# Wide attention of a fused transformer kernel: products of 128 rows by 128 columns gathered in every other slot

## The chip, the cores and the metric

The kernel runs on one core of a Trainium2 chip. The time is the device time of one execution in microseconds; smaller is better. A core has TensorE (matrix products; its weight loads run beside them), VectorE, ScalarE, GpSimd and SyncE, each with its own queue that it works through in program order. They wait for each other through semaphores.

## The reference, cut to what matters

Six layers are computed on x of 16 x 256 x 128. The change touches only the first, an attention with 16 heads of 64:

```python
q = (x @ Wq).reshape(b, s, N_HEADS, HEAD_DIM)
k = (x @ Wk).reshape(b, s, N_HEADS, HEAD_DIM)
v = (x @ Wv).reshape(b, s, N_HEADS, HEAD_DIM)
dot = jnp.einsum('bihd,bkhd->bhik', q, k)
w = jax.nn.softmax(dot / jnp.sqrt(jnp.float32(HEAD_DIM)), axis=-1)
a = jnp.einsum('bhij,bjhd->bihd', w, v)
a = a.reshape(b, s, N_HEADS * HEAD_DIM)
return a @ Wo + bo
...
x = x + _L0_attn_a_ref(_layernorm(x, axis=-1), L0_attn_a_Wq, L0_attn_a_Wk, L0_attn_a_Wv, L0_attn_a_Wo, L0_attn_a_bo)
```

## The kernel before

The wide attention takes the 16 batches one after the other, and the 16 heads of a batch as 8 pairs. A batch has 8 slots, one for each pair, and `wide_slots` lists what stands in a slot as (name, index, batches ahead). `wide_walk` repeats this list for all batches, and every engine walks through the same list in the same order and does its own part of each entry. So the order of this one list is the order of every queue. The entries are:

- norm: TensorE turns the normalized x of a batch (two transposes, 128x128), ScalarE copies them out. xn is ScalarE's normalizing ahead of it.
- qk: queries and keys of one pair, two float32 products with w_q and w_k, each in two passes, 128 rows by 128 columns; ScalarE copies both (128x512) to the SBUF, and GpSimd makes a bfloat16 copy for "max".
- v: a quarter of the values (128x128, 512 wide), copied out by ScalarE.
- max: approximate scores in bfloat16 (64 rows by 128 columns), of which VectorE takes the row maxima. split and turnmax: VectorE splits the maxima of a batch in three bfloat16 parts, TensorE turns them (128x128), VectorE copies the result to `shift`. The first score of the batch waits for this copy.
- score: the shift (`pick` times `shift`) and the exact scores (64x128), then ScalarE's exponential; GpSimd adds the two key tiles.
- value and sum: products of 128 rows by 64 columns into the banks Ob; divide: VectorE's reciprocal and multiplication.
- project: eight products with w_o (128x128; float32, so 16 passes), which VectorE adds to x, and takes the moments for the next layer.

The entries norm, qk, v, project and turnmax share the two PSUM banks 6 and 7, strictly in turn: the bank is the entry's place in the list modulo 2. A filling waits until the filling before it in the same bank has been copied out (`drained`).

```python
    for what, i, _ in slots:
        if what in ("norm", "qk", "v", "project", "turnmax"):
            bank[what, i] = len(bank) % 2
```

In a slot i the list has: divide of pair i-2, score of pair i, max of pair i+1 of the next batch, value and sum of pair i-1, and then the 128x128 products; slot 6 has the split behind its max, and slot 7 the turnmax and its products ahead of value and sum. On VectorE the two additions of the projections stand in slots 3 and 5, each behind that slot's divide and maximum.

Of the kernel before, what the change touches and what calls it, by code (L numbers as in the profile page):

```python
# [243 lines left out]
PAIRS = H // 2  # L244
# [1684 lines left out]
def wide_slots():  # L1929
    slots = []  # L1930
    for i in range(PAIRS):
        slot = [("divide", (i - 2) % PAIRS, -1 if i < 2 else 0), ("score", i, 0)]
        slot += [("max", (i + 1) % PAIRS, 2 if i + 1 >= PAIRS else 1)]
        slot += [("split", 0, 1)] if i == 6 else []
        slot += [("turnmax", 0, 1)] if i == 7 else []
        products = [("qk", (i + 3) % PAIRS, 2 if i + 3 >= PAIRS else 1)]
        products += {1: [("v", 0, 1)], 2: [("v", 1, 1), ("xn", 0, 2)], 3: [("project", 0, -1)],
                     4: [("v", 2, 1), ("norm", 0, 2)], 5: [("project", 1, -1)], 6: [("v", 3, 1)]}.get(i, [])
        values = [(what, (i - 1) % PAIRS, -1 if i < 1 else 0) for what in ("value", "sum")]
        slots += slot + (products + values if i == 7 else values + products)  # L1940
    return slots


def wide_walk():

    slots, order, counts = wide_slots(), [], [0, 0]
    bank = {}
# [3 lines that stand above are left out]
    for n in range(-2, NB + 1):  # L1951
        for what, i, ahead in slots:
            if 0 <= n + ahead < NB:
                m = bank.get((what, i))
                if m is not None:
                    counts[m] += 1
                order.append((what, i, n + ahead, m, counts[m] if m is not None else None))
    return order
# [376 lines left out]
```

## Time and profile before

| | us |
|---|---|
| median of 3 runs | 2353.46 (2351.25 to 2359.56) |
| the profiled execution | 2350.0 |
| its span in the trace | 2348.3 |
| TensorE busy in the span | 2052.1 (87%) |
| VectorE busy | 1544.7 (66%) |
| ScalarE busy | 1199.0 (51%) |
| GpSimd busy | 825.0 (35%) |

Busy times are sums over six layers with different limits, so that they say little about one of them. The wide attention is read from stretches within its first 655 us. Matmul ends are modelled in the trace, so distances are taken from start to start. "128*64 128x256" in a row is a matmul of 128 rows by 64 columns of the array with 256 columns streamed. "x8" means that eight instructions in a row were merged, and what stands in brackets is the idle time before them and who ended it.

### The profile page before, as it was taken

The page shows a single profiled execution, that of the slowest core. Times are in us where ns is not written, and L with a number is a line of the kernel's source. Part 1 is how long each engine was busy: PE and PEld are TensorE (multiplying, and loading weights), DVE is VectorE, ACT ScalarE, POOL GpSimd, SP SyncE. Part 2 cuts the span into 40 slices and gives each one's busy share as a digit, 9 for nine tenths or more (in the row PEclk, how much of TensorE's full clock was granted, in tenths as well). Part 3 has the DMA queues.
Part 4 walks back from the last instruction along what each step waited for, and adds up shares of the span by engine and source line. Part 5 has one row for each costly group of instructions (what it writes and reads, how often), then busy time and mean ns, then how long its engine had stood idle before and what let it go on. Part 6 is the DMA issues. An engine that isn't in the chain of part 4 may idle for free. (4 is left out here: it accounts for less than half of the span.)

```text
span 2348.3 us, 52692 instructions
## 1 busy us (share of the span) xinstructions
PE 2052.1 (87%) x20735; PEld 1381.5 (59%) x20735; DVE 1544.7 (66%) x2742; ACT 1199.0 (51%) x2044; POOL 825.0 (35%) x1272
## 2 busy tenths in 40 slices
PE   6999999999959997998689989997599985479996
PEld 3666666666648995555578966664345543335553
DVE  5777777777743435666354447774688875768884
ACT  3444444444343324665623326655477776447774
POOL 4444444444423432332144414441233322433330
PEclk9999999999969998999789989998699997769998
DMA  5000000000000022444000214441244420134441
GB/s 167 1 1 1 1 1 1 1 1 1 1 6 2 14 46 70 113 113 99 2 4 1 55 29 113 113 112 32 70 100 115 113 61 1 42 80 107 113 109 46
DMA packets 142787, 120.97 MB, mean 52 GB/s; under 512 B 11808, under 2 KB 127408, under 8 KB 142548
## 3 DMA queue, kind: packets, MB, share of 16 engines
q1 hardware_dynamic: 142548, 117.64, 21.1%
q8 instruction: 167, 2.74, 0.5%
q14 instruction: 72, 0.59, 0.1%
HBM read 63.48 MB, written 54.12 MB: 50 GB/s over the span
## 5 line engine op out<-in xcount | busy, mean ns | idle before, releaser
L906 DVE TENSOR_REDUCE l_group_mx<-maxima 128x4 f32<-128x1024 f32 x248 | 304.0, 1226 | 69.0 <-PE maxima L699 67.5
L834 ACT ACTIVATE l_group_pr<-scores 128x1024 f32<-128x1024 f32 x256 | 261.5, 1021 | 71.7 <-PE scores L720 69.1
L2171 POOL TENSOR_TENSOR l_wide_tiles_sum<-l_wide_pr 128x256 f32<-128x256 f32 x256 | 180.7, 727 | 212.4 <-ACT l_wide_pr L2114 212.4
L2142 DVE RECIPROCAL l_wide_rc<-bank 128x256 f32<-128x256 f32 x128 | 223.8, 1749 | 8.4 <-PE bank L2075 7.9
L2114 ACT ACTIVATE l_wide_pr<-scores 128x512 f32<-128x512 f32 x256 | 139.1, 595 | 163.1 <-PE scores L2058 163.1
L2126 DVE TENSOR_REDUCE l_wide_mx<-maxima 128x2 f32<-128x512 f32 x248 | 159.4, 685 | 52.6 <-PE maxima L2038 52.0
L906 DVE TENSOR_REDUCE l_slope_mx<-maxima 128x6 f32<-128x768 f32 x124 | 118.9, 959 | 74.2 <-PE maxima L706 72.7
L2104 ACT ACTIVATE l_wide_qk<-bank 128x512 f32<-128x512 f32 x128 | 76.4, 597 | 175.2 <-PE bank L2025 175.2
L906 DVE TENSOR_REDUCE l_rope_mx<-maxima 128x6 f32<-128x768 f32 x124 | 118.8, 958 | 56.3 <-PE maxima L706 55.4
L834 ACT ACTIVATE l_slope_pr<-scores 128x768 f32<-128x768 f32 x128 | 103.5, 809 | 87.0 <-PE scores L727 86.8
L834 ACT ACTIVATE l_rope_pr<-scores 128x768 f32<-128x768 f32 x128 | 103.7, 811 | 77.0 <-PE scores L727 76.8
L740 PE MATMUL bank<-l_group_pr,va 128*32 128x256 f32 x2048 | 142.1, 397 | 0.0
L2069 PE MATMUL bank<-l_wide_pr,l_wide_va 128*64 128x256 f32 x1024 | 138.8, 392 | 0.0
L699 PE MATMUL maxima<-l_group_st 50*128 50x256 bf16 x992 | 101.8, 285 | 39.1 <-DVE l_group_mx L906 14.4
L2058 PE MATMUL scores<-l_wide_qk 64*128 64x256 f32 x1024 | 131.4, 376 | 0.0
L2166 POOL CAST l_wide_qk<-l_wide_qk 128x512 bf16<-128x512 f32 x128 | 78.1, 610 | 146.2 <-ACT l_wide_qk L2104 146.2
L1001 POOL CAST l_group_cols<-l_group_mx 128x32 bf16<-128x32 f32 x32 | 6.7, 209 | 318.8 <-DVE l_group_mx L906 318.8
L720 PE MATMUL scores<-l_group_st 53*128 53x256 bf16 x1024 | 102.6, 279 | 16.3 <-ACT l_group_pr L834 11.5
L2058 PEld LDWEIGHTS scores<-l_wide_qk 64*128 64x128 f32 x1024 | 98.6, 189 | 9.8
L1660 ACT ACTIVATE l_rope_e_ht<-maxima 128x512 f32<-128x512 f32 x64 | 38.2, 597 | 106.4 <-PE maxima L1612 106.0
L2025 PE MATMUL bank<-l_wide_xnt,w_q 128*128 128x256 f32 x256 | 90.3, 435 | 2.5 <-ACT l_wide_qk L2104 1.4
L1660 ACT ACTIVATE l_slope_e_ht<-maxima 128x512 f32<-128x512 f32 x64 | 38.2, 597 | 104.4 <-PE maxima L1612 104.1
(468 smaller groups left out, 4853.5 us busy)
## 6 DMA issues: line engine op xcount, KB each, us to landing
l_group_st<-stack_dram SPq DMA_DIRECT2D x64, 384.0 KB, 5.5
l_slope_st<-stack_dram SPq DMA_DIRECT2D x32, 384.0 KB, 5.6
l_rope_st<-stack_dram SPq DMA_DIRECT2D x32, 384.0 KB, 5.5
stack_dram<-l_group_parts SPq DMA_DIRECT2D x64, 192.0 KB, 2.3
stack_dram<-l_group_parts SPq DMA_DIRECT2D x64, 128.0 KB, 1.9
stack_dram<-l_slope_parts SPq DMA_DIRECT2D x32, 192.0 KB, 2.4
stack_dram<-l_rope_parts SPq DMA_DIRECT2D x32, 192.0 KB, 2.3
stack_dram<-l_slope_parts SPq DMA_DIRECT2D x32, 128.0 KB, 2.3
```

Of the source, the lines that this page charges most:

```text
L699: ins = pe.matmul(Mx[:, z, first:first + keys], st[at, b % KEEP, 0, i, t * P:(t + 1) * P], st[at, b % KEEP, 1, i, 0:keys], start=(t == 0 o ...
L720: ins = pe.matmul(Tp[:, z, t * S:t * S + S - first], st[at, b % KEEP, 1, i, t * P:(t + 1) * P], st[at, b % KEEP, 0, i, first:S], start=(t ...
L740: ins = pe.matmul(Ob[i // 2][32 * z:32 * z + 32, (i % 2) * S + first:(i % 2) * S + S], va[:, b % KEEP, t, h // G, :], pr[:, (h // 2) % AHE ...
L834: act.activation(pr[:, i % AHEAD, :, 0:keys], Tp[:, :, 0:keys], ACT.Exp).then_inc(s["exps"], 1)
L906: dve.tensor_reduce(mx[:, b % 2, :, :, i], max_bank(i, b)[:, :, 0:BLOCKS * keys].rearrange("p z (a k) -> p z a k", k=keys), AX.X, ALU.max, ...
L2025: ins = pe.matmul(bank[:, z * S:(z + 1) * S], w[:, i * P:(i + 1) * P], xnt[:, at, :], start=True, stop=True)
L2058: ins = pe.matmul(Tb[z][:, t * S:(t + 1) * S], qk[rows(z), at, i, 1, t * P:(t + 1) * P], qk[rows(z), at, i, 0, :], start=False, stop=(t == ...
L2069: ins = pe.matmul(Ob[i % 2][rows(z), 0:S], va[:, at, kt, 2 * i + z, :], pr[:, i % 2, z, kt * S:(kt + 1) * S], start=(kt == 0), stop=(kt == ...
L2114: act.activation(pr[:, i % 2, z, :], Tb[z][:], ACT.Exp).then_inc(s["exps"], 1)
L2126: dve.tensor_reduce(mx[:, at, :, 2 * i + z], max_banks(i, b)[z][:].rearrange("p (t k) -> p t k", k=S), AX.X, ALU.max, negate=True).then_in ...
L2142: own.done(dve.reciprocal(rc[:], Ob[i % 2][:, S:2 * S]))
L2171: pool.tensor_tensor(tiles_sum[:, i % 2, z, :], pr[:, i % 2, z, 0:S], pr[:, i % 2, z, S:2 * S], ALU.add).then_inc(s["added"], 1)
```

## The change

The list of `wide_slots` is written differently. Slots 1, 3 and 5 have no qk, v, norm or project any more, nor has slot 7 a qk. Slots 0, 2, 4 and 6 have the qk of two pairs each. The normalizing for two batches ahead moves from slot 2 to slot 0, the quarters of v from slots 1, 2, 4 and 6 to 0, 2, 4 and 6, and both projections of the batch before, from slots 3 and 5, to slot 6: one as the first product of the row, the other as the last. Nothing else is changed; each engine has as many instructions as before. The changed file is four lines longer, so that its line numbers behind this place are higher by 4.

```diff
--- before.py
+++ after.py
@@ -1933,9 +1933,13 @@
         slot += [("max", (i + 1) % PAIRS, 2 if i + 1 >= PAIRS else 1)]
         slot += [("split", 0, 1)] if i == 6 else []
         slot += [("turnmax", 0, 1)] if i == 7 else []
-        products = [("qk", (i + 3) % PAIRS, 2 if i + 3 >= PAIRS else 1)]
-        products += {1: [("v", 0, 1)], 2: [("v", 1, 1), ("xn", 0, 2)], 3: [("project", 0, -1)],
-                     4: [("v", 2, 1), ("norm", 0, 2)], 5: [("project", 1, -1)], 6: [("v", 3, 1)]}.get(i, [])
+
+        products = []
+        if i % 2 == 0:
+            products = [("qk", j % PAIRS, 2 if j >= PAIRS else 1) for j in (i + 3, i + 4)]
+            products = {0: [("xn", 0, 2), ("v", 0, 1)] + products, 2: products[0:1] + [("v", 1, 1)] + products[1:2],
+                        4: [("norm", 0, 2), ("v", 2, 1)] + products, 6: [("project", 0, -1), ("v", 3, 1)] + products}[i]
+            products = (products + [("project", 1, -1)]) if i == 6 else products
         values = [(what, (i - 1) % PAIRS, -1 if i < 1 else 0) for what in ("value", "sum")]
         slots += slot + (products + values if i == 7 else values + products)
     return slots
```

TensorE, from the end of slot 5 to slot 7 of a batch, before (l0_wide_xnt with w_q and w_k is qk, w_v with it is v, w_o is the projection, parts the turned maxima, pr and tiles_sum are value and sum), beginning with the projection in slot 5:

```order
L2083 MATMUL bank7<-w_o,l0_wide_att_t 128x128 x8
L2054 MATMUL scores<-l0_wide_shift,pick 128x512 x2
L2058 MATMUL scores<-l0_wide_qk 128x256 x4
L2038 MATMUL maxima<-l0_wide_qk16 128x256 x4
L2069 MATMUL bank5<-l0_wide_pr,l0_wide_va 64x256 x4
L2075 MATMUL bank5<-l0_wide_tiles_sum,ones 64x256 x2
L2025 MATMUL bank6<-l0_wide_xnt,w_q 128x256
L2025 MATMUL bank6<-l0_wide_xnt,w_k 128x256
L2031 MATMUL bank7<-w_v,l0_wide_xnt 128x512
L2054 MATMUL scores<-l0_wide_shift,pick 128x512 x2
L2058 MATMUL scores<-l0_wide_qk 128x256 x4
L2038 MATMUL maxima<-l0_wide_qk16 128x256 x4
```

And in the change, slot 6, from behind its "sum" up to slot 7's first value product:

```order
L2087 MATMUL bank6<-w_o,l0_wide_att_t 128x128 x8
L2035 MATMUL bank7<-w_v,l0_wide_xnt 128x512
L2029 MATMUL bank6<-l0_wide_xnt,w_q 128x256
L2029 MATMUL bank6<-l0_wide_xnt,w_k 128x256
L2029 MATMUL bank7<-l0_wide_xnt,w_q 128x256
L2029 MATMUL bank7<-l0_wide_xnt,w_k 128x256
L2087 MATMUL bank6<-w_o,l0_wide_att_t 128x128 x8
L2058 MATMUL scores<-l0_wide_shift,pick 128x512 x2
L2062 MATMUL scores<-l0_wide_qk 128x256 x4
L2042 MATMUL maxima<-l0_wide_qk16 128x256 x4
L2050 MATMUL bank7<-ident16,parts 128x128 x2
L2073 MATMUL bank4<-l0_wide_pr,l0_wide_va 64x256 x4
```

Before, one projection stands in slot 5, slot 6 has the two products of a qk and a v, and the scores of slot 7 follow the v; behind the turn of parts came slot 7's qk. In the change the row of slot 6 has both projections with v and two qk between, the second projection stands directly ahead of slot 7, and slot 7 has no qk behind the turn of parts.

VectorE, slots 5 to 7, before (TENSOR_TENSOR x is the addition of a projection, RECIPROCAL with the line after it the divide, maxima the maximum, shift the copy that the next batch's score waits for), beginning with that addition in slot 5:

```order
L2148 TENSOR_TENSOR x<-x,bank7 128x128
L2150 BN_STATS moments<-x 128x6
L2142 RECIPROCAL l0_wide_rc<-bank4 128x256
L2143 TENSOR_TENSOR l0_wide_att_t<-bank4,l0_wide_rc 128x256
L2126 TENSOR_REDUCE l0_wide_mx<-maxima 128x2 x2
L2132 CAST parts<-l0_wide_mx 128x4x16
L2133 TENSOR_TENSOR l0_wide_mrest<-l0_wide_mx,parts 128x32
L2134 CAST parts<-l0_wide_mrest 128x4x16
L2135 TENSOR_TENSOR parts<-l0_wide_mrest,parts 128x4x16
L2142 RECIPROCAL l0_wide_rc<-bank5 128x256
L2143 TENSOR_TENSOR l0_wide_att_t<-bank5,l0_wide_rc 128x256
L2126 TENSOR_REDUCE l0_wide_mx<-maxima 128x2 x2
```

And in the change, beginning with the last instruction of the split in slot 6:

```order
L2139 TENSOR_TENSOR parts<-l0_wide_mrest,parts 128x4x16
L2152 TENSOR_TENSOR x<-x,bank6 128x128
L2154 BN_STATS moments<-x 128x6
L2152 TENSOR_TENSOR x<-x,bank6 128x128
L2154 BN_STATS moments<-x 128x6
L2146 RECIPROCAL l0_wide_rc<-bank5 128x256
L2147 TENSOR_TENSOR l0_wide_att_t<-bank5,l0_wide_rc 128x256
L2130 TENSOR_REDUCE l0_wide_mx<-maxima 128x2 x2
L2142 COPY l0_wide_shift<-bank7 128x256
L2146 RECIPROCAL l0_wide_rc<-bank4 128x256
```

The addition that stood ahead of slot 6's divide stands now, with the other one, behind slot 6's split; the divide, the maximum and the copy to shift of slot 7 follow it.

## Rows read from the trace of the kernel before

**Rows 1.** Busy time by stretch; columns: stretch, its length, busy us and instructions, clock, DMA
```profile
core 0: us, PE busy (x) PEld busy (x) DVE busy (x) ACT busy (x) POOL busy (x), PEclk, DMA share, GB/s
100.00:200.00 100.00, 99.34 (x736) 64.14 (x733) 77.28 (x110) 42.89 (x79) 43.42 (x65) 1.00 0.00 1
```

**Rows 2.** Timeline of TensorE, slots 5 (end), 6 and 7; start us, length us
```profile
302.62 1.95 PE L2083 MATMUL bank<-w_o,l_wide_att_t 128*128 128x128 f32 x16
304.50 0.39 PE L2054 MATMUL scores<-l_wide_shift,pick 64*128 64x512 bf16 x2
...
305.90 1.08 PE L2069 MATMUL bank<-l_wide_pr,l_wide_va 128*64 128x256 f32 x8
...
307.35 0.70 PE L2025 MATMUL bank<-l_wide_xnt,w_q 128*128 128x256 f32 x2
307.88 0.59 PE L2025 MATMUL bank<-l_wide_xnt,w_k 128*128 128x256 f32 x2
308.31 1.02 PE L2031 MATMUL bank<-w_v,l_wide_xnt 128*128 128x512 f32 x2
309.27 0.39 PE L2054 MATMUL scores<-l_wide_shift,pick 64*128 64x512 bf16 x2
...
310.79 0.65 PE L2025 MATMUL bank<-l_wide_xnt,w_q 128*128 128x256 f32 x2
...
311.80 1.08 PE L2069 MATMUL bank<-l_wide_pr,l_wide_va 128*64 128x256 f32 x8
312.72 0.60 PE L2075 MATMUL bank<-l_wide_tiles_sum,ones 128*64 128x256 f32 x4
313.54 0.39 PE L2054 MATMUL scores<-l_wide_shift,pick 64*128 64x512 bf16 x2 [0.22 <-DVE l_wide_shift L2138]
```

**Rows 3.** Timeline of TensorE, the next batch's first score
```profile
352.46 0.39 PE L2054 MATMUL scores<-l_wide_shift,pick 64*128 64x512 bf16 x2 [0.22 <-DVE l_wide_shift L2138]
```

**Rows 4.** Timeline of VectorE, slots 6 and 7
```profile
304.67 0.29 DVE L2148 TENSOR_TENSOR x<-x,bank 128x128 f32<-128x128 f32 x1 [3.07 <-PE bank L2083]
...
305.20 1.74 DVE L2142 RECIPROCAL l_wide_rc<-bank 128x256 f32<-128x256 f32 x1
...
308.63 0.20 DVE L2132 CAST parts<-l_wide_mx 128x64 bf16<-128x64 f32 x1
...
309.89 1.74 DVE L2142 RECIPROCAL l_wide_rc<-bank 128x256 f32<-128x256 f32 x1
...
313.20 0.28 DVE L2138 COPY l_wide_shift<-bank 128x256 bf16<-128x256 bf16 x1
```

**Rows 5.** Timelines of ScalarE, weight loads (PEld) and TensorE around a transpose, slot 2
```profile
336.70 0.60 ACT L2104 ACTIVATE l_wide_qk<-bank 128x512 f32<-128x512 f32 x1 [1.56 <-PE bank L2025]
...
337.35 0.20 PEld L2019 LDWEIGHTS bank<-ident,l_wide_xn 128*128 128x128 f32 x2 [0.66 <-ACT l_wide_qk L2104]
...
336.50 1.02 PE L2031 MATMUL bank<-w_v,l_wide_xnt 128*128 128x512 f32 x2
337.36 0.43 PE L2019 MATMUL bank<-ident,l_wide_xn 128*128 128x128 f32 x2
337.72 0.39 PE L2054 MATMUL scores<-l_wide_shift,pick 64*128 64x512 bf16 x2
```

**Rows 6.** Timeline of TensorE in the last batch, without products
```profile
622.13 0.39 PE L2054 MATMUL scores<-l_wide_shift,pick 64*128 64x512 bf16 x2 [0.52 <-DVE l_wide_shift L2138]
...
624.23 0.60 PE L2075 MATMUL bank<-l_wide_tiles_sum,ones 128*64 128x256 f32 x4
624.76 0.39 PE L2054 MATMUL scores<-l_wide_shift,pick 64*128 64x512 bf16 x2
```

**Rows 7.** Waits of TensorE in the fill, 20 to 50 us; total us, times, longest
```profile
PE bank L2025 <- ACT l_wide_qk L2104: 1.4, 3, 0.7
PE bank L2025 <- ACT l_wide_xnt L2101: 0.9, 2, 0.5
```

**Rows 8.** Timeline of TensorE at the end of the fill
```profile
43.93 0.39 PE L2038 MATMUL maxima<-l_wide_qk 64*128 64x256 bf16 x4
...
45.90 0.39 PE L2054 MATMUL scores<-l_wide_shift,pick 64*128 64x512 bf16 x2
```

## The prediction

> **What bounds the kernel now.** I read three views in this order. First the busy time of each engine over stretches of the span: while the wide attention runs, TensorE has work in 99.3 us of 100, at the full granted clock, and VectorE in 77, ScalarE and GpSimd in 43 each [rows 1]. So this layer, the first 655 us of the 2348.3 us span, goes at TensorE's pace; DMA is idle in it, and nothing behind it is touched by the diff. Second the timeline of TensorE over the end of one batch [rows 2]. One batch takes 38.92 us, from 313.54 to 352.46 [rows 2, 3]. The reader is to see which blocks follow with a gap. A slot is "score" with "max" 1.40 us (304.50 to 305.90), "value" with "sum" 1.45 (305.90 to 307.35), then the products of 128x128. Third VectorE's timeline [rows 4]: from 304.67 on no row shows a pause, and the copy of the turned maxima at 313.20 is what TensorE waits for: the score products of the next batch start only at 313.54.
>
> **What a change of shape costs.** A block of w_q products lasts 0.53 us where it is the first behind a 64-column product (307.35 to 307.88), and the w_k block, the same size, 0.43 [rows 2]. So entry costs 0.10: the load of weights had no matmul of its own kind to hide under. A v block lasts 0.86 us before another 128x128 product (336.50 to 337.36) and 0.96 before a score (308.31 to 309.27) [rows 2, 5]: leaving costs 0.10. "sum" lasts 0.53 before a score too when nothing stands between (624.23 to 624.76, no wait) [rows 6], against 0.43 for its four products as a w_k block has them, so that step from 128x64 to 64x128 costs the same 0.10. The Trainium skill, TensorEngine Tiling (Array Packing), section Key Properties, says that a change of tiling mode drains the engine; the trace agrees, at 0.10 us a time.
>
> **The change, step by step, for one batch.** Slots 1, 3 and 5 lose their 128x128 products. Each then goes "sum" to "score" directly, and one entry and one leaving are gone: 3 x 0.20 = -0.60 us. The products themselves are all still there.
> Slot 7 keeps the turn of the maxima but loses its qk: those took 1.01 us (310.79 to 311.80) where 0.86 is the bare time and 0.10 the leaving, which stays: -0.05.
> The old wait in front of slot 0: "sum" has 0.82 us there where 0.53 would do (slot 7 lasts 4.27 us, 309.27 to 313.54; its parts are 1.52 for score, max and turn, 309.27 to 310.79, then 1.01 and 1.45, in sum 3.98): -0.29 [rows 2].
> New late weight loads. The products have two banks, taken in turn, and in slots 0, 2, 4 and 6 a third product now needs a bank that ScalarE has just emptied, with only one product of 0.86 us between. The trace has this pattern once a batch: ScalarE ends its copy at 337.30, the load of weights starts at 337.35 and the matmul at 337.36, which is just where it would have been [rows 5]. So no full wait comes, but the load has no lead, and a load without lead costs a 128x128 float32 product 0.10, as at the entry. With a lead of 0.01 to 0.02 I take 0.09 for each of four: +0.36 (bounds 0 and 0.40). The old case was a transpose, whose block is 0.36 (337.36 to 337.72) with 0.10 of leaving, where two passes of 0.11 (a projection is 16 such in 1.78) would be bare: 0.05 is saved there, and 0.05 as the transpose now takes the entry: -0.10. In slot 6 the fifth product has a longer row ahead of it and is free.
> A price by the page alone: the Trainium skill, TensorE: Matmul & The Clock Gate, section LDWEIGHTS, gives columns / 1.2 ns, which is 107 ns for 128 columns; with it the four would be 0.43 instead of 0.36.
>
> **The moved projections.** This is the step that decides. VectorE adds the two projections to x in program order. Before, they stood in slots 3 and 5, and VectorE sat 3.07 us ahead of each [rows 4], with time to catch up. Now both stand in slot 6, the second as the last product of it. VectorE finishes the first, and then must wait about 4 us (v and two qk, 0.86 each, and the second projection, 1.88 with the leaving from 302.62 to 304.50, so 1.78) with the divide of pair 5 behind it, whose operands lie ready. Behind that divide stand the maximum and the copy of the turned maxima, for which TensorE's next batch waits. I count from the start of slot 7, where the second projection is just done. Its add starts 0.17 later (304.67 against 304.50); add and statistics 0.53 (to 305.20); divide and maximum 3.31 (309.89 to 313.20); copy to TensorE's start 0.34 (to 313.54) [rows 2, 4]. Sum 4.35 us. TensorE's own slot 7 is then 1.52 + 0.10 (leaving the turn) + 1.45 = 3.07. So it waits 4.35 - 3.07 = +1.28 us ahead of slot 0.
>
> Elsewhere VectorE has cover: a pair costs it 3.31 us, an odd slot is now 1.40 + 1.45 = 2.85, but an even one 5.6 or more, and the next slot's divide never has to be done before the slot after. ScalarE's two exponentials (1.1 us a slot) and GpSimd's sums keep pace in such short slots: 624.76 is 2.63 us behind the score before it without a wait (622.13 and 624.76) [rows 6].
>
> Sum for a batch: -0.60 - 0.05 - 0.29 + 0.36 - 0.10 + 1.28 = **+0.60 us**. It holds for 13 batches (those with a projection in them and two batches ahead to fill): +7.8 us.
>
> **The edges.** Fill before the first score: TensorE waited 1.4 + 0.9 us there for ScalarE's copies [rows 7], 0.7 of it because two qk in a row took the same bank, which now alternate; with other products between, I take the 2.3 as gone, and 0.8 for four switches less (4 x 0.20). Against it: from the last "max" of the fill to the first score (43.93 to 45.90) [rows 8] VectorE's maximum and copy hid a qk of 0.9 us, now nothing. -2.3 + 0.9 - 0.8 = -2.2 (bounds -4 and 0; a clock that rises earlier or later is not counted). First batch, without projections and without the wait: -0.4. The last two: fewer switches and a shorter VectorE chain: -1.0. Edges: -3.6.
>
> **Total** +7.8 - 3.6 = +4.2 us on the profiled execution's 2350.0: 2354.2. Its 2350.0 lies 3.5 below the median of the three runs, 2353.46; with that, I predict 2357.7 us. What a measurement of this kernel can tell from no change is about 0.3%, 7.1 us.
>
> **Rivals.**
> A. The gain without the price: VectorE is done with the divide of pair 5 in time, so that slot 7 has no wait. For it: VectorE is busy only 77% [rows 1]. Against it: the order of its queue, in which nothing passes the second projection. A batch would be -0.60 - 0.05 - 0.29 + 0.36 - 0.10 = -0.68, in all -8.8 - 3.6 = -12.4: 2341. Chance 0.08. The Trainium skill, TensorEngine Tiling (Array Packing), section Key Properties, by which each change of mode that falls away is a drain less, speaks for this case and not for the wait.
> B. Slower, past 0.3%: VectorE is late for the first projection as well. It can start the divide of pair 4 0.1 into slot 6 ("sum" of slot 5 ends 1.40 + 0.92 + 0.60 into it), and has 3.31 and 1.26 to do (the split of the maxima, 308.63 to 309.89) [rows 4]: free at 4.7. The first projection is ready for it at 5.0 (2.85 + 0.10 + 1.78, and 0.27 for the end of its last product), and its bank is wanted again at 5.6, when the add of 0.29 is done. So there are 0.3 us to spare; every tenth beyond costs TensorE a tenth in every batch. With ScalarE's copies also late by 0.1 in four places it is +0.5 a batch: +6.5, 2364. Decides from 0.3 us of lateness. Chance 0.24.
> C. The late loads cost nothing (TensorE's queue holds the load back less than at an entry): +0.24 a batch, +3.1 - 3.6 = -0.5: 2353. Chance 0.16.
> D. The change does not remove switches: excluded by the order of rows and by 624.23 to 624.76 [rows 6].
> My forecast has 0.52.
>
> **How the numbers follow.** The forecast itself spreads by the fill (2 us either way) and by three runs that differ among themselves by 8 us. From +4.2 with such a spread (about 4 us) a quarter of its 0.52 passes +7.1, which is 0.13; with nearly all of B's 0.24 less 0.06 that stay inside, slower is 0.31. Faster is A and a little of C: 0.11. Within 0.3%: 0.58. The range leaves out A and the far end of B: 2347 to 2366.
>
> **What would show each step.** In the changed profile: a wait of TensorE at the first score product of a batch on VectorE's copy of shift, "idle before" 1.2 us (0.22 now), 14 times; a wait of VectorE of about 4 us ahead of one add to x in each batch, the other nearly none; odd slots of 2.85 us; no wait at the third product of a row, but its first pass 0.1 us longer; a batch of 39.5 us against 38.92; a first score at about 44 instead of 45.90. A batch under 38.5 us would prove A, one over 40 B. The prediction is wrong in its main step if VectorE's idle time ahead of its second add does not exceed 3 us.

## The result, and the profile after

The changed kernel takes 2360.78 us (median of 20 runs, 2352.96 to 2365.99), the kernel before 2354.07 (20 runs, 2349.57 to 2363.78). The medians differ by 6.7 us. The ratio of the means (2360.40 and 2354.96) is 1.0023, with a 95% interval of 1.0013 to 1.0034: 5.4 us more (3.1 to 8.0), within the 0.3% that were called no change, but clear of zero. The profiled execution has a span of 2360.4 us.

The busy shares in the layer have fallen, TensorE's from 99.3 [rows 1] to 96.3 us in 100, at the full clock:

```profile
core 0: us, PE busy (x) PEld busy (x) DVE busy (x) ACT busy (x) POOL busy (x), PEclk, DMA share, GB/s
100.00:200.00 100.00, 96.33 (x722) 62.88 (x721) 72.25 (x107) 41.64 (x78) 41.81 (x62) 1.00 0.00 1
```

TensorE's timeline from the end of slot 6 to the first score of the next batch, and the score one batch later:

```profile
308.26 1.95 PE L2087 MATMUL bank<-w_o,l_wide_att_t 128*128 128x128 f32 x16
310.14 0.39 PE L2058 MATMUL scores<-l_wide_shift,pick 64*128 64x512 bf16 x2
...
311.55 0.28 PE L2050 MATMUL bank<-ident,parts 128*128 128x128 bf16 x2
311.76 1.08 PE L2073 MATMUL bank<-l_wide_pr,l_wide_va 128*64 128x256 f32 x8
312.67 0.60 PE L2079 MATMUL bank<-l_wide_tiles_sum,ones 128*64 128x256 f32 x4
314.50 0.39 PE L2058 MATMUL scores<-l_wide_shift,pick 64*128 64x512 bf16 x2 [1.22 <-DVE l_wide_shift L2142]
```

```profile
354.04 0.39 PE L2058 MATMUL scores<-l_wide_shift,pick 64*128 64x512 bf16 x2 [1.22 <-DVE l_wide_shift L2142]
```

The first score waits 1.22 us where it waited 0.22 [rows 2]; slot 7 lasts 4.36 us (310.14 to 314.50), and a batch 39.54 (314.50 to 354.04) instead of 38.92. VectorE, the same place:

```profile
305.85 0.29 DVE L2152 TENSOR_TENSOR x<-x,bank 128x128 f32<-128x128 f32 x1 [0.54 <-PE bank L2087]
...
310.32 0.29 DVE L2152 TENSOR_TENSOR x<-x,bank 128x128 f32<-128x128 f32 x1 [3.85 <-PE bank L2087]
...
310.85 1.74 DVE L2146 RECIPROCAL l_wide_rc<-bank 128x256 f32<-128x256 f32 x1
...
314.16 0.28 DVE L2142 COPY l_wide_shift<-bank 128x256 bf16<-128x256 bf16 x1
```

Its first addition of a projection finds the engine idle for 0.54 us, the second for 3.85. From the second on, it has no pause: 0.53 us to the divide at 310.85, 3.31 to the copy at 314.16, 0.34 to the score. That answers to [rows 4], where the same chain began one slot earlier. Over 13 batches, the waits (total us, times, longest) are:

```profile
DVE x L2152 <- PE bank L2087: 57.0, 26, 3.8
...
PE scores L2058 <- DVE l_wide_shift L2142: 15.9, 13, 1.2
```

The third product in slot 0, whose bank ScalarE has just emptied, and the qk ahead of it:

```profile
318.31 0.59 PE L2029 MATMUL bank<-l_wide_xnt,w_q 128*128 128x256 f32 x2
318.74 0.59 PE L2029 MATMUL bank<-l_wide_xnt,w_k 128*128 128x256 f32 x2
319.17 0.69 PE L2029 MATMUL bank<-l_wide_xnt,w_q 128*128 128x256 f32 x2
319.69 0.59 PE L2029 MATMUL bank<-l_wide_xnt,w_k 128*128 128x256 f32 x2
320.22 0.39 PE L2058 MATMUL scores<-l_wide_shift,pick 64*128 64x512 bf16 x2
```

The first w_q block lasts 0.43 us (318.31 to 318.74), the second 0.52 (319.17 to 319.69). The second one's load of weights starts at 319.15, when ScalarE's copy of v is done, 0.02 us ahead of its matmul; the next block's starts 0.21 us ahead (319.48 for 319.69). No idle time is reported, only the longer block: this is the late weight load. Slots 2, 4 and 6 have one such block each. In slots 4 and 6 it is the fourth product and not the third, as there v stands second and its copy frees the fourth product's bank.

The fill (the products ahead of the first score) ended earlier, and the last batch later. First score after the fill (45.90 before [rows 8]):

```profile
43.53 0.39 PE L2058 MATMUL scores<-l_wide_shift,pick 64*128 64x512 bf16 x2 [0.93 <-DVE l_wide_shift L2142]
```

The last projections, and the granted clock and busy times of their stretches:

```profile
645.14 2.05 PE L2087 MATMUL bank<-w_o,l_wide_att_t 128*128 128x128 f32 x16
647.64 2.05 PE L2087 MATMUL bank<-w_o,l_wide_att_t 128*128 128x128 f32 x16 [0.45 <-DVE x L2152]
...
657.22 0.49 PE L2087 MATMUL bank<-w_o,l_wide_att_t 128*128 128x128 f32 x2 [1.36 <-DVE l_wide_att_t L2147]
658.16 3.66 PE L2087 MATMUL bank<-w_o,l_wide_att_t 128*128 128x128 f32 x16 [0.45 <-DVE x L2152]
```

```profile
658.00:662.00 4.00, 3.66 (x16) 3.47 (x16) 0.47 (x3) 0.00 (x0) 0.00 (x0) 0.57 0.00 0
```

In the last two places the second projection waits 0.45 us for VectorE's addition of the first. The very last one runs at a granted clock of 0.57 (0.50, which is 1.2 GHz, from 659 to 661 us) and takes 3.66 us where the others take 2.05. The next layer's first instruction on VectorE is at 664.05 us, before the change at 656.55:

```profile
664.05 0.21 DVE L212 TENSOR_TENSOR mean<-moments 128x32 f32<-128x32 f32 x1 [1.50 <-PEq L2298]
```

```profile
656.55 0.21 DVE L212 TENSOR_TENSOR mean<-moments 128x32 f32<-128x32 f32 x1 [1.70 <-PEq L2294]
```

So the layer is 7.5 us longer in these two executions. What lies behind it is untouched by the change, and took 1696.4 us after (2360.4 - 664.05) and 1691.8 before.

### The profile page after: what moved, and what is told of

Its sections match the earlier page's. It is cut to its first block and busy times, and to the rows that moved or that the text cites. A ratio compares the mean times of both kernels' runs of the same rounds, so it can differ in the third digit from the quotient of the medians.

```text
span 2360.4 us, 52692 instructions
## 1 busy us (share of the span) xinstructions
PE 2046.0 (87%) x20735; PEld 1380.4 (58%) x20735; DVE 1537.7 (65%) x2742; ACT 1201.7 (51%) x2044; POOL 825.9 (35%) x1272
## 5 line engine op out<-in xcount | busy, mean ns | idle before, releaser
L2073 PEld LDWEIGHTS bank<-l_wide_pr,l_wide_va 128*64 128x64 f32 x1024 | 62.1, 136 | 45.4 <-issue 24.6
```

The lines of the kernel that those rows point to most:

```text
L2073: ins = pe.matmul(Ob[i % 2][rows(z), 0:S], va[:, at, kt, 2 * i + z, :], pr[:, i % 2, z, kt * S:(kt + 1) * S], start=(kt == 0), stop=(kt == ...
```

## The experiments

A batch is measured as in [rows 2, 3], from a first score to the next one, in the middle of the layer; it was the same to 0.01 us in all 13 inner batches of each kernel but the one of the turn behind the late projection, where the first of them was shorter. The table has them all; the middle column is the layer, up to the next layer's first VectorE instruction.

| kernel | a batch, us | end of the layer, us | time |
|---|---|---|---|
| before | 38.92 | 656.6 | 2354.07 |
| the change | 39.55 | 664.1 | ratio 1.0023 (1.0013 to 1.0034) |
| adjacent projections | 38.26 | 645.8 | ratio 0.9942 (0.9928 to 0.9957) |
| projections alone, adjacent | 38.63 | 650.9 | ratio 0.9973 (0.9960 to 0.9985) |
| projections alone, split | 39.09 | 656.9 | one run, 2355.4 |
| half v copies | 39.37 | 659.8 | one run, 2363.4 |
| turn in slot 6 | 38.15 | 643.7 | ratio 0.9939 (0.9916 to 0.9963) |
| turn behind the late projection | 38.56 | 649.2 | one run, 2346.6 |
| projections back | 38.65 | 650.3 | one run, 2348.1 |
| one switch added | 38.36 | 647.4 | one run, 2350.8 |

The single times scatter by several us, in stages that no edit touches; what a single run shows is its batch.

**Adjacent projections.** Against the change:

```diff
-                        4: [("norm", 0, 2), ("v", 2, 1)] + products, 6: [("project", 0, -1), ("v", 3, 1)] + products}[i]
-            products = (products + [("project", 1, -1)]) if i == 6 else products
+                        4: [("norm", 0, 2), ("v", 2, 1)] + products, 6: [("project", 0, -1), ("project", 1, -1), ("v", 3, 1)] + products}[i]
```

> The changed kernel with one thing different: in slot 6 the second projection stands directly behind the first, ahead of v and the two qk, and no longer as the last product of the row. Theory (VectorE is held at its second addition to x, and the divide, maximum and copy of shift queue behind it): VectorE's addition now comes 2.4 us before slot 7, its wait ahead of it falls from 3.85 to about 1.3 us, the copy of shift is done 2.97 us into slot 7 where TensorE needs 3.07, so the wait of 1.22 us at the first score of a batch goes to 0. A batch goes from 39.55 to 38.26 us, the two projections have different banks so that the last batch loses its 0.45 us waits as well, and the whole is 12 us under the kernel before: ratio 0.995. Rival 1 (the wait comes from the amount of VectorE's work in the short slots 5 to 7, not from its order): the batch stays at 39.4 to 39.55 us and the ratio at 1.002. Rival 2 (the gathered products do not save anything, the whole difference is in the projections): the batch comes back to 38.9 us, ratio 1.000.

Measured: a batch of 38.26 us and a ratio of 0.9942. VectorE and TensorE around slot 7:

```profile
303.05 0.29 DVE L2151 TENSOR_TENSOR x<-x,bank 128x128 f32<-128x128 f32 x1 [1.17 <-PE bank L2086]
...
303.58 1.74 DVE L2145 RECIPROCAL l_wide_rc<-bank 128x256 f32<-128x256 f32 x1
...
308.26 0.28 DVE L2141 COPY l_wide_shift<-bank 128x256 bf16<-128x256 bf16 x1
```

```profile
305.55 0.39 PE L2057 MATMUL scores<-l_wide_shift,pick 64*128 64x512 bf16 x2
...
308.62 0.39 PE L2057 MATMUL scores<-l_wide_shift,pick 64*128 64x512 bf16 x2
```

The second addition waits 1.17 us instead of 3.85, the divide starts at 303.58, before slot 7 begins (305.55), and slot 7 lasts 3.07 us without a wait. The whole 1.29 us are gone with the place of one product, with the same products on all engines. Both rivals fall: the amount of work is the same, and the batch is 0.66 us under that of before.

**Projections alone, adjacent.** Against the kernel before:

```diff
-        products += {1: [("v", 0, 1)], 2: [("v", 1, 1), ("xn", 0, 2)], 3: [("project", 0, -1)],
-                     4: [("v", 2, 1), ("norm", 0, 2)], 5: [("project", 1, -1)], 6: [("v", 3, 1)]}.get(i, [])
+        products += {1: [("v", 0, 1)], 2: [("v", 1, 1), ("xn", 0, 2)], 4: [("v", 2, 1), ("norm", 0, 2)]}.get(i, [])
+        products = [("project", 0, -1), ("project", 1, -1), ("v", 3, 1)] + products if i == 6 else products
```

> The kernel before (a qk in every slot, v where they were) with only the two projections moved: both as the first two products of slot 6. It has no gathering of the other products, but lacks the projections' own later place behind the qk. Theory: every switch of shape stays, as slots 3 and 5 still have a qk; VectorE is no longer late for the copy of shift, so the wait of 0.29 us ahead of slot 0 goes, and nothing else. A batch of 38.63 us against 38.92; about 4 us less in all, ratio 0.998. Rival (the projections are what matters, and gathering does nothing): a batch as short as that of the adjacent projections with gathering, 38.3 us. Together with that kernel it gives the worth of the gathering alone: the theory has 38.63 - 38.26 = 0.37 us a batch (0.60 + 0.05 - 0.36 + 0.10 by the prediction's terms).

Measured: 38.63 us a batch. Slot 7 of one:

```profile
306.89 0.39 PE L2054 MATMUL scores<-l_wide_shift,pick 64*128 64x512 bf16 x2
...
310.88 0.39 PE L2054 MATMUL scores<-l_wide_shift,pick 64*128 64x512 bf16 x2
```

3.99 us and no wait: only the old wait of 0.29 us is gone. So of the 0.66 us that adjacent projections with gathering have over the kernel before, 0.29 are this wait and 0.37 the gathering, as expected.

**Projections alone, split.** The same, with the second projection at the end of slot 6:

```diff
-        products = [("project", 0, -1), ("project", 1, -1), ("v", 3, 1)] + products if i == 6 else products
+        products = [("project", 0, -1), ("v", 3, 1)] + products + [("project", 1, -1)] if i == 6 else products
```

> The kernel before (a qk in every slot) with only the projections moved, as the change has them: one as the first product of slot 6, one as its last. Theory: VectorE's chain into slot 7 is the same 4.35 us as in the change, but TensorE's slot 7 still has its qk and lasts 3.98 us, so the wait ahead of slot 0 is 0.37 us where it was 0.29, and one late weight load adds 0.09: a batch of 39.09 us. So the place of the projections alone costs 0.2 us a batch, and it is the lost qk in slot 7 that lays the other 0.9 us of the wait bare. Rival (a projection at the end of the row costs its 1.2 us by itself): a batch of 40.1 us.

Measured: 39.09 us. Slot 7:

```profile
308.04 0.39 PE L2054 MATMUL scores<-l_wide_shift,pick 64*128 64x512 bf16 x2
...
312.39 0.39 PE L2054 MATMUL scores<-l_wide_shift,pick 64*128 64x512 bf16 x2 [0.30 <-DVE l_wide_shift L2138]
```

It lasts 4.35 us, as VectorE's chain does, and the wait in it is a small one, as slot 7's qk covers the rest. Against the adjacent projections, the late one costs 0.46 us in this neighbourhood (39.09 for 38.63): 0.36 in slot 7, and 0.09 of a late weight load in slot 6 (8.43 us for 8.34). In the change it costs 1.29 (39.55 for 38.26). The 1.29 need both edits, the late place and a slot 7 without its qk.

**Half v copies.** Against the change, from the third batch on; the kernel then leaves out half of each v, and the values there are those of an earlier batch:

```diff
-                    act.activation(va[:, at, i // 2, 8 * (i % 2):8 * (i % 2) + 8, :].rearrange("p h d -> p (h d)"),
-                                   Mb[m][:], ACT.Copy).then_inc(drained[m], 1)
+                    heads = 8 if b < 2 else 4
+                    act.activation(va[:, at, i // 2, 8 * (i % 2):8 * (i % 2) + heads, :].rearrange("p h d -> p (h d)"),
+                                   Mb[m][:, 0:64 * heads], ACT.Copy).then_inc(drained[m], 1)
```

> The changed kernel, but from the third batch on ScalarE copies only the first 4 of 8 heads of each v block out of its bank (256 columns instead of 512), so that half of the values stay those of an earlier batch; everything else is as in the change. Theory of the late weight loads: in slots 0, 4 and 6 the bank of the third product is then free 0.2 us earlier, its weight load has its lead, and its block falls from 0.52 to 0.43 us; slot 2, where the bank is freed by a qk's copy, keeps 0.52. A batch of 39.28 us against 39.55, with the wait of 1.22 us unchanged. Rival (the 0.52 us are the price of a third product in a row, whatever its bank): 0.52 everywhere and 39.55 us.

Measured: 39.37 us, a saving of 0.18 and not 0.27. The third product in slot 0:

```profile
317.49 0.59 PE L2029 MATMUL bank<-l_wide_xnt,w_k 128*128 128x256 f32 x2
317.92 0.59 PE L2029 MATMUL bank<-l_wide_xnt,w_q 128*128 128x256 f32 x2
318.36 0.59 PE L2029 MATMUL bank<-l_wide_xnt,w_k 128*128 128x256 f32 x2
```

Its w_q block (317.92 to 318.36) is down to 0.44. Slot 0 is 5.63 us (5.72 in the change), slot 4 5.81 (5.90), slot 2 unchanged at 5.73, as expected; slot 6 is 9.29 (9.30). There the last projection waits on the bank of the product two ahead of it: once the fourth product is not late any more, the fifth is (the projection's block is 1.97 us instead of 1.88). The waits of weight loads show it, as a line that the change does not have (total us, times, longest):

```profile
PEld bank L2087 <- ACT l_wide_qk L2108: 2.9, 13, 0.2
```

So the rival falls, and the price belongs to the chain of banks, not to a place in the row.

**Turn behind the late projection.** Against the change, with the line that puts turnmax in slot 7 taken out:

```diff
-        slot += [("turnmax", 0, 1)] if i == 7 else []
...
-            products = (products + [("project", 1, -1)]) if i == 6 else products
+            products = (products + [("project", 1, -1), ("turnmax", 0, 1)]) if i == 6 else products
```

> The changed kernel with its late second projection left where it is, and only the turn of the maxima moved from slot 7 to behind that projection, at the end of slot 6's row. VectorE is held at its second addition just as in the change, but the copy of shift now stands directly behind it, ahead of the divide and the maximum of 3.31 us. Theory (the path is addition, divide, maximum, copy, in this order): the wait of 1.22 us at the first score goes; in its place the maximum of slot 7 is done about 1.25 us into slot 0 where TensorE's next max wants it at 1.09, a new wait of 0.2 us there. A batch of 38.4 us against 39.55. Rival (VectorE's idle 3.85 us is lost work that TensorE must wait for somewhere): a batch above 39.2 us.

Measured: 38.56 us a batch. VectorE is held for 3.85 us just as in the change, and TensorE no longer pays for it at the score, but at the max of slot 0:

```profile
305.35 0.29 DVE L2151 TENSOR_TENSOR x<-x,bank 128x128 f32<-128x128 f32 x1 [3.85 <-PE bank L2086]
...
305.88 0.27 DVE L2141 COPY l_wide_shift<-bank 128x256 bf16<-128x256 bf16 x1
...
308.19 1.28 DVE L2129 TENSOR_REDUCE l_wide_mx<-maxima 128x2 f32<-128x512 f32 x2
```

```profile
305.28 0.39 PE L2057 MATMUL scores<-l_wide_shift,pick 64*128 64x512 bf16 x2
...
308.13 0.39 PE L2057 MATMUL scores<-l_wide_shift,pick 64*128 64x512 bf16 x2
...
309.62 0.40 PE L2041 MATMUL maxima<-l_wide_qk 64*128 64x256 bf16 x4 [0.23 <-DVE l_wide_mx L2129]
```

The copy of shift (305.88) is now done before the divide (306.07), the score starts at 308.13 without a wait, and the max of slot 0 waits 0.23 us for the maximum of slot 7. It is 0.16 us a batch more than the expected 38.4: that max starts at 309.62 where 309.22 would do (308.13 plus the 1.09 of a score), so this wait costs 0.40, of which the profile counts 0.23 as idle.

**Turn in slot 6.** The same move, made to the kernel of adjacent projections:

```diff
-        slot += [("turnmax", 0, 1)] if i == 7 else []
...
-                        4: [("norm", 0, 2), ("v", 2, 1)] + products, 6: [("project", 0, -1), ("project", 1, -1), ("v", 3, 1)] + products}[i]
+                        4: [("norm", 0, 2), ("v", 2, 1)] + products, 6: [("project", 0, -1), ("project", 1, -1), ("v", 3, 1)] + products + [("turnmax", 0, 1)]}[i]
```

> The kernel with adjacent projections, and the turn of the maxima moved from slot 7 to the end of slot 6's row, so that slot 7 has no 128x128 product. Theory: one leaving less (0.10 us), and at most 0.05 given back as the transpose's weight load comes late; the copy of shift leaves the path. VectorE waits for the turn with the divide of pair 5 behind it again, about 2 us, but that divide and the maximum are now wanted only in the next slot 0, at 1.09 us into it. A batch of 38.16 to 38.21 us against 38.26, about 1 us in all, which is within what a comparison can tell from none; ratio 0.9938. Rival (holding the divide of pair 5 costs TensorE wherever the copy of shift stands): a wait of 0.5 to 1 us in slot 0 and a batch of 39 us.

Measured: 38.15 us a batch and a ratio of 0.9939, against 0.9942 with the turn in slot 7; the two intervals overlap, so that only the batches tell them apart. VectorE now waits 2.1 us for the turn in every batch, and no line of TensorE's own stands among the waits:

```profile
DVE l_wide_shift L2140 <- PE bank L2048: 27.4, 13, 2.1
```

An idle stretch of VectorE is free as long as what is queued behind it is not wanted.

**Projections back.** Against the change:

```diff
-                        4: [("norm", 0, 2), ("v", 2, 1)] + products, 6: [("project", 0, -1), ("v", 3, 1)] + products}[i]
-            products = (products + [("project", 1, -1)]) if i == 6 else products
+                        4: [("norm", 0, 2), ("v", 2, 1)] + products, 6: [("v", 3, 1)] + products}[i]
+        products = {3: [("project", 0, -1)], 5: [("project", 1, -1)]}.get(i, products)
```

> The changed kernel with the two projections put back where they were before the change, in slots 3 and 5; qk, v and norm stay gathered in the even slots. So only slot 1 has no 128x128 product. Theory: of the three switches saved one is left (-0.20 us), slot 7's -0.05 stays, the late weight loads stay (+0.26 net), and VectorE's chain fits nearly or wholly into slot 7 (wait 0 to 0.25 us, was 0.29). A batch of 38.65 to 38.9 us: as much as before the change. So the gathering has to include the projections to be worth anything. Rival (the gathering of qk alone brings the gain): 38.3 us.

Measured: 38.65 us, at the lower end. Slot 7:

```profile
306.10 0.39 PE L2058 MATMUL scores<-l_wide_shift,pick 64*128 64x512 bf16 x2
...
309.16 0.39 PE L2058 MATMUL scores<-l_wide_shift,pick 64*128 64x512 bf16 x2
```

3.06 us, no wait. The gathering of qk alone is worth little; by the terms its own part is -0.20, -0.05 and +0.26, together nothing, and the 0.27 us under the kernel before are the old wait of 0.29.

VectorE does not keep up here because slot 6 is longer: slots 6 and 7 together are 8.79 us (5.73 + 3.06), and before, without the wait, they were 8.75 (4.77 + 3.98). What is shorter is the end of the split. Before, and here:

```profile
309.32 0.64 DVE L2135 TENSOR_TENSOR parts<-l_wide_mrest,parts 128x64 bf16<-128x64 f32 x1
309.89 1.74 DVE L2142 RECIPROCAL l_wide_rc<-bank 128x256 f32<-128x256 f32 x1
```

```profile
305.20 0.23 DVE L2139 TENSOR_TENSOR parts<-l_wide_mrest,parts 128x64 bf16<-128x64 f32 x1
305.34 1.75 DVE L2146 RECIPROCAL l_wide_rc<-bank 128x256 f32<-128x256 f32 x1
```

The split's last instruction holds the divide behind it for 0.57 us before (309.32 to 309.89) and for 0.14 here (305.20 to 305.34). VectorE had no pause from that slot 6 on to the copy of shift, so these 0.43 us stood on the path, and they are more than the old wait of 0.29. Before, GpSimd's cast of a qk ran beside this instruction; here none does. That the cast is the cause was not tried alone.

**One switch added.** Against adjacent projections, v 1 leaves slot 2 and stands alone in slot 1:

```diff
-            products = {0: [("xn", 0, 2), ("v", 0, 1)] + products, 2: products[0:1] + [("v", 1, 1)] + products[1:2],
+            products = {0: [("xn", 0, 2), ("v", 0, 1)] + products, 2: products,
...
+        products = [("v", 1, 1)] if i == 1 else products
```

> The kernel with adjacent projections, with one v block moved out of slot 2's row into slot 1, where it stands alone: one entry and one leaving more in every batch (+0.20 us), but slot 2 then has only two products and no late weight load (-0.09). Theory: slot 1 3.91 instead of 2.85 us, slot 2 4.77 instead of 5.73, a batch of 38.37 us against 38.26. Rival (a switch costs nothing by itself, what counted was the number of products in a row): 38.17 us or less.

Measured: 38.36 us, 0.10 more, with slot 1 at 3.91 us and slot 2 at 4.77. Slot 1:

```profile
315.06 0.39 PE L2058 MATMUL scores<-l_wide_shift,pick 64*128 64x512 bf16 x2
...
318.96 0.39 PE L2058 MATMUL scores<-l_wide_shift,pick 64*128 64x512 bf16 x2
```

A switch costs its 0.20 even where it saves a late load, and the rival that would have had the batch shorter falls.

## Why the prediction was right, point by point

- The forecast was 4.2 us more, within what counts as no change; 5.4 us were measured (ratio 1.0023). Right in direction, and right that the gain of fewer switches is given back by a wait. The sum for a batch is right term by term; the sum for the edges of the layer is not, as the last points say, and that the total comes so near is in part luck.
- A batch was to take 0.60 us more; it takes 0.63, 13 times, which is 8.2 us for 7.8 (of the waits of 1.2 us there are 13 too, where the signs named 14). The wait ahead of slot 0 was to cost 1.28; slot 7 of the change lasts 4.36 us and slot 7 of adjacent projections 3.07, so it costs 1.29. Its cause was the queue of VectorE behind the second addition: shown twice, by moving the projection, and by moving the copy of shift ahead of the divide with the projection left in place.
- The switches: -0.60 for three. One switch put back costs 0.10 net of a late load of 0.09, so 0.19 to 0.20. The gathering as a whole was worth 0.37 (38.63 against 38.26), the sum of the terms -0.60, -0.05, +0.36 and -0.10 being -0.39. The prediction took the old wait of 0.29 as gone without saying why it was there: the end of the split lasted 0.43 us longer in the kernel before, which is more than the wait (see projections back).
- The late loads: 0.09 in each of four slots, no idle time reported, fifth product free. All as measured, but that in slots 4 and 6 the late product is the fourth. (The transpose of [rows 5], which served as the model, stands in slot 4, not in slot 2.) That the fifth becomes late when the fourth is not, was not foreseen in the expectation of the half copies, though it follows from the same rule. The Trainium skill, TensorE: Matmul & The Clock Gate, section LDWEIGHTS, gives the columns divided by 1.2 as the ns of a load, from which 107 ns are an estimate for 128 columns; the trace agrees, with 0.09 to 0.10 us for a load that had next to no lead.
- Rival A (no wait) and rival C (free late loads) fall by the rows above. Rival B (VectorE late for the first projection too) falls by the 0.54 us that it sat idle ahead of it; the split took 0.9 us there and not the 1.26 of [rows 4], so that there was more room than the 0.3 us counted.
- The fill was to save 2.2 us and saved 2.4 (43.53 for 45.90), but not by the terms of the forecast. TensorE's reported waits in it were to fall from 2.3 us to 0.9; they are 2.3 before and 2.1 in the change (0.5 and 0.4 us still for ScalarE, 0.4 for GpSimd, 0.9 for the copy of shift). Another part is TensorE's pace: at the start of the fill a w_k block took 0.86 us (22.73 to 23.59) instead of 0.43, though the profile gives the granted clock as 1.00 there. The last slow block ended at 26.94 in the change and at 29.48 before. By my estimate from the blocks the slow ones cost 2.4 us in the change and 3.2 before. The prediction had set this aside as not counted. The kernel of projections split, which gathers nothing, has its first score at 43.63 as well: there the first two qk fall into different banks, and the slow blocks end at 24.89. With adjacent projections, where the gathering is that of the change, it comes at 45.35, and the first two qk share a bank (a wait of 0.69). So the 2.4 us do not show what the gathering does to the fill, and that the number fits is luck.
- The first batch was to save 0.4, and saved 0.45 (33.70 for 34.15).
- The term that was mis-sized is the end: "The last two: fewer switches and a shorter VectorE chain: -1.0". The last but one saved 0.77 (35.40 for 36.17), but the last one with the rest of the layer took 2.9 us more (37.32 for 34.42, from its first score to the next layer): +2.1 for -1.0. The step that I left out is the bank: with no v and no qk between them the two projections fall into the same bank, and the second waits for VectorE's addition of the first. Two other kernels have these two waits of 0.45 us, the turn behind the late projection and the half v copies, whose end has the order of the change; the last batch takes 35.7 us in both. With adjacent projections it takes 34.3, and 34.3 too with the projections split alone: in both the two lie in two banks. So about 1.4 us are the bank.
- The other 1.6 us of the end are the fall of the clock, which in this execution met the last projection (3.66 against 2.05 us). In the turn behind the late projection the granted clock was full over the last projection (from 644.90 us on):

```profile
643.10:647.00 3.90, 2.54 (x18) 2.16 (x18) 1.35 (x4) 0.00 (x0) 0.00 (x0) 1.00 0.02 4
```

  It was full too in the half v copies, where the last projection took 2.05 us. So the fall does not follow from this order alone; how often the change meets it was not measured. All edges together came to -0.7 us in the profiled execution, and to -2.3 without the fall, where -3.6 were forecast.
- The profiled execution is 12.1 us longer than that of before, of which the layer explains 7.5. The other 4.6 lie in stages that are the same in both kernels. In the ten profiled executions those stages took between 1691.3 us (projections alone, adjacent: 2342.2 - 650.9) and 1701.8 (half v copies: 2361.6 - 659.8); what in them differs stays open. The 20 runs do not carry the whole 7.5 us of the layer: their means differ by 5.4 us. How often the fall of the clock is in them is not known.

## What to carry to other kernels

When products are gathered to save changes of the array's shape, count for each consumer queue what stands behind the wait for the last product: one addition that waited 3.9 us held a divide, a maximum and a copy, and the copy was what the next batch needed. Place a product whose consumer has other urgent work behind it early in a row, or put the urgent consumer ahead in the queue. With two banks in turn, a product whose bank is emptied just in time (here the third or fourth of a row) shows no wait and still pays 0.09 us for its late weight load, and at the ends of a loop the products that kept two fillings apart are missing.

## What the runs showed of the hardware that was not expected

- A weight load that begins together with its matmul shows no idle time on TensorE: it shows as a w_q block (two passes) of 0.52 us instead of 0.43.
- A wait that the profile counts as 0.23 us idle cost 0.40 in starts, in the max of slot 0; the one of 1.22 us cost 1.29. The ends of matmuls are modelled, so starts are the measure.
- The granted clock fell to 0.57 over the last projection's stretch in one execution and stayed full in two other kernels' with the same waits ahead of it (1.36 and 0.45 us).
- VectorE's last instruction of the split took 0.64 us where GpSimd's cast of qk ran beside it (309.32 in the kernel before, in 13 batches alike), and 0.23 in the changed order (305.09), where none did. In the kernel before it was on the path, with 0.43 us to the next start more; in the change VectorE sat idle behind it.
